# A selective scan's input: scaled by GpSimd and transposed by TensorE, in place of matmuls with a diagonal matrix

## The reference, cut to what matters

```python
x_conv = silu(causal_conv(x_in))                      # [16, 256, 256]
Bm, Cm = jnp.split(x_conv @ W_xp + b_xp, 2, axis=-1)  # 16 states each
delta = softplus(x_conv @ W_dt + b_dt)
dA  = jnp.exp(delta[..., None] * A)                   # decay
dBx = (delta * xc)[..., None] * Bm[:, :, None, :]     # drive: u times B
h = dA_t * h + dBx_t                                  # for each token t
y_t = jnp.einsum('bds,bs->bd', h, C_t)
y = y + D_skip * xc;  y = y * silu(z)
out = y @ W_out + b_out                               # then the layer norms
x = x + layernorm(x_quantized @ w_quantized.T + bias) # after a maximum over all of x
```

## Time and profile before

| | |
|---|---|
| three runs | 677.97, 679.1 and 680.75 us, median 679.1 |
| the profiled execution | 680.76 us, its span 679.0 us |
| mean granted clock of TensorE | 0.909 |
| the slots | 44.1 us to about 607 us; all but the first about 72.6 us each |
| from the end of the last scans to the end | about 72 us |
| VectorE in the slots | nine tenths busy |

### The profile page before, as it was taken

The page is one execution under the profiler, slowest core; times in us unless marked ns, Lnnn a source line. Parts: engine busy times, 40 slices in busy tenths (PEclk is TensorE's granted clock), DMA queues, the critical chain, the costliest instruction groups (busy, mean ns, idle before and its releaser), DMA issues.

```text
span 679.0 us, 10276 instructions
## 1 busy us (share of the span) xinstructions
PE 559.0 (82%) x2893; PEld 429.9 (63%) x2893; DVE 576.2 (85%) x1106; ACT 416.4 (61%) x814; POOL 322.5 (47%) x331
## 2 busy tenths in 40 slices
PE   4889999997999799986999699979997887773371
PEld 3467787775777577775777567767776776662120
DVE  4057898899998989899989998999989998985595
ACT  2447875785667757776478457765777654621364
POOL 3033554545555536455454654553655545431264
PEclk7979999997999899998999799989999899987555
DMA  7000000000000000000000000000000000000012
GB/s 208 9 1 1 0 1 1 1 0 1 1 1 1 0 2 0 0 0 0 0 0 0 0 1 0 0 0 0 0 0 0 1 1 0 1 1 0 0 47 77
DMA packets 9959, 6.20 MB, mean 9 GB/s; under 512 B 2624, under 2 KB 8896, under 8 KB 9920
## 3 DMA queue, kind: packets, MB, share of 16 engines
q1 hardware_dynamic: 9920, 5.78, 3.1%
HBM read 3.68 MB, written 2.10 MB: 9 GB/s over the span
## 4 chain that ended last, share of the span: by engine, by line
PE 42%; DVE 33%; issue 14%; ACT 5%; POOL 4%; DVEq 1%; DMA 0%; POOLq 0%; ACTq 0%
PE drive L951 16%; DVE state L1162 12%; PE hT L967 8%; PE fbank L894 7%; DVE acc_d L1185 4%; PE fbank L910 2%; PE bbank L985 2%; DVE delta L1145 2%; DVE acc_d L1182 2%; DVE yv L1191 1%; PE drive L894 1%; DVE yg L1196 1%; DVE bst L1205 1%; POOL state L592 1%; ACT h L622 1%
## 5 line engine op out<-in xcount | busy, mean ns | idle before, releaser
L1162 DVE TENSOR_TENSOR_SCAN state<-decay,drive 128x512 f32<-128x512 f32 x256 | 297.1, 1201 | 19.4 <-PE drive L951 18.2
L951 PE MATMUL drive<-diag,uT 128*128 128x256 f32 x1024 | 253.4, 392 | 1.6 <-DVE state L1162 1.0
L951 PEld LDWEIGHTS drive<-diag,uT 128*128 128x128 f32 x1024 | 193.2, 199 | 29.1 <-issue 3.3
L711 ACT ACTIVATE decay<-delta,a_neg 128x510 f32<-128x510 f32 x256 | 169.5, 723 | 20.3 <-DVE state L1162 19.2
L967 PE MATMUL hT<-ident,state 128*128 128x128 f32 x1024 | 147.4, 284 | 36.6 <-DVE acc_d L1185 35.3
L967 PEld LDWEIGHTS hT<-ident,state 128*128 128x128 f32 x1024 | 122.6, 147 | 67.5 <-issue 51.6
L729 ACT ACTIVATE term<-hT,Ct 128x256 f32<-128x256 f32 x256 | 102.6, 478 | 55.3 <-PE hT L967 55.3
L497 POOL TENSOR_SCALAR_AFFINE_SELECT diag<-Bt 128x512 f32<-128x512 f32 x128 | 98.1, 776 | 61.4 <-PE drive L951 40.8
L1185 DVE SCALAR_TENSOR_TENSOR acc_d<-hT,Ct,acc_d 128x256 f32<-128x256 f32 x224 | 92.2, 467 | 0.9 <-PE hT L967 0.9
L512 POOL TENSOR_TENSOR acc<-acc,term 128x512 f32<-128x512 f32 x48 | 61.1, 1272 | 46.6 <-ACT term L729 46.6
L527 POOL TENSOR_TENSOR bstd<-bvar,minus_half 128x4 f32<-128x4 f32 x16 | 16.3, 1017 | 107.2 <-DVE bvar L1253 62.6
(11 more groups left out here) (165 smaller groups left out, 613.3 us busy)
## 6 DMA issues: line engine op xcount, KB each, us to landing
out_dram<-state SPq DMA_DIRECT2D x8, 256.0 KB, 2.2
x_all<-in_L_attn_x_dram SPq DMA_DIRECT2D x2, 256.0 KB, 4.5
state<-in_L_attn_conv_w_dram SPq DMA_DIRECT2D x1, 512.0 KB, 5.8
w_in<-in_L_attn_W_in_dram SPq DMA_DIRECT2D x1, 256.0 KB, 3.1
w_dt<-in_L_attn_W_dt_dram SPq DMA_DIRECT2D x1, 256.0 KB, 5.0
w_out<-in_L_attn_W_out_dram SPq DMA_DIRECT2D x1, 128.0 KB, 3.5
w_ffn<-in_L_ffn_weight_dram SPq DMA_DIRECT2D x1, 64.0 KB, 2.6
bout_r<-in_L_attn_b_out_dram SPq DMA_DIRECT2D x1, 64.0 KB, 3.3
```

The lines of the kernel that those rows point to most:

```text
L711: last = nc.scalar.activation(decay[:, g % DECAYS, h, :, s, 1:], delta[:, par, h, :, 1:], ACT.Exp, scale=a_neg[:, h, SG * g + s:SG * g + s ...
L951: last = nc.tensor.matmul(dst[:, :, P * c:P * c + P], uT[:, par, TC * b + c, P * h:P * h + P], diag[:, n % DIAGS, c, :, :], start=True, st ...
L1162: nc.vector.tensor_tensor_scan(state[:, n % STATES, h, :, :].rearrange("p s t -> p (s t)"), decay[:, g % DECAYS, h, b, :, :].rearrange("p ...
```

## The change

The diag(B) blocks go. GpSimd now multiplies `uT` itself by B: for each unit four tensor_scalar instructions of 128 x 256 (two halves of time, two states), with one value of B for each partition. The result, `scaled`, has time on the partitions, four buffers as before. TensorE transposes it with the identity, 8 transposes of 128 x 128 for a unit, straight into the drive buffers. GpSimd therefore waits for `uT` before a pair's first unit, and ScalarE must not overwrite `uT` before the last unit of its old pair has been scaled. `scaled` is twice as large as `diag`; `term` goes from four buffers to two. All four step tables are set anew.

```diff
-DECAYS, DIAGS, STATES, TERMS = 2, 4, 4, 4
+DECAYS, SCALED, STATES, TERMS = 2, 4, 4, 2
...
-POOL_STEPS = dict(front_root=(0,), front_residual=(19,), sum_states=(8,), back_root=(15, 21, 26))
+POOL_STEPS = dict(front_root=(3,), front_residual=(23,), sum_states=(6,), back_root=(13, 21, 26))
...
-                 front_uT=(42, 46), back_norms=(33, 41, 47))
+                 front_uT=(45, 45), back_norms=(33, 41, 47))
...
                 if n == 0:
                     pool.wait_ge(bc_ready, nth(pr, 3, 2))
-
-                old = trailing(pr, par, n, DIAGS)
+                    pool.wait_ge(uT_ready, nth(pr, 2, 2))
+
+                old = trailing(pr, par, n, SCALED)
...
-                b_cols = Bt[:, par, g, b, :, :].rearrange("p c s -> p (c s)").unsqueeze(2).to_broadcast([P, TC * SG, P])
-                nc.gpsimd.affine_select(out=diag[:, n % DIAGS, :, :, :].rearrange("p c s t -> p (c s) t"), in_=b_cols,
-                                        compare_op=ALU.is_equal, fill=0.0, base=0, pattern=[[0, TC * SG], [-1, P]],
-                                        channel_multiplier=1).then_inc(diag_ready, 1)
+                for c in range(TC):
+                    for s in range(SG):
+                        last = nc.gpsimd.tensor_scalar(scaled[:, n % SCALED, c, s, :], uT[:, par, TC * b + c, :],
+                                                       Bt[:, par, g, b, c, s:s + 1], None, ALU.mult)
+                last.then_inc(scaled_ready, 1)
...
             def front_uT(pr, par, k):
                 act.wait_ge(front_full, nth(pr, 9, 8 + k))
+                if pr.after(2):
+                    act.wait_ge(scaled_ready, nth(pr.plus(-1), UNITS, 0))
...
-                    dst = drive[:, n % 2, h, :].rearrange("p (s t) -> p s t", s=SG)
                     for c in range(TC):
-                        last = nc.tensor.matmul(dst[:, :, P * c:P * c + P], uT[:, par, TC * b + c, P * h:P * h + P],
-                                                diag[:, n % DIAGS, c, :, :], start=True, stop=True)
+                        for s in range(SG):
+                            last = nc.tensor.transpose(drive[:, n % 2, h, L * s + P * c:L * s + P * c + P],
+                                                       scaled[:, n % SCALED, c, s, P * h:P * h + P], ident[:, :])
```

More of the change, by code:

```diff
@@ L75 @@
 ROUND_AT = 1.5 * 2.0 ** 20
-POOL_STEPS = dict(front_root=(0,), front_residual=(19,), sum_states=(8,), back_root=(15, 21, 26))
-ACT_STEPS = dict(front_xin=(5, 10), silu_table=(21,), front_silu=(21, 22, 23), exp_table=(23,),
-                 front_norm=(16,), front_xnT=(23,), front_dt=(29, 30), front_exp=(35,), front_log=(35,),
-                 front_uT=(42, 46), back_norms=(33, 41, 47))
[L86 to L90, removed]
+POOL_STEPS = dict(front_root=(3,), front_residual=(23,), sum_states=(6,), back_root=(13, 21, 26))
+ACT_STEPS = dict(front_xin=(7, 11), silu_table=(21,), front_silu=(21, 22, 23), exp_table=(23,),
+                 front_norm=(14,), front_xnT=(23,), front_dt=(27, 31), front_exp=(35,), front_log=(35,),
+                 front_uT=(45, 45), back_norms=(33, 41, 47))
+PE_STEPS = dict(front_in=(1, 6, 17, 21), front_transpose=(23,), front_dt=(24, 28), front_bc=(36,),
+                front_ut=(41, 41), back_y=(12, 15), back_out=(20,), back_transpose=(46,))
+DVE_STEPS = dict(front_stats=(0,), front_shift=(3,), front_low=(21,), front_bc=(24,), front_delta=(24,),
+                 front_u=(25,), back_y=(8, 10), back_gate=(11,), back_norms=(11, 13, 15, 21, 24, 27, 29),
+                 back_amax=(30,), back_h2T=(30,))
 def due(steps, name, at):
@@ L212, in build_sandwich @@
         decay = sb("decay", [P, DECAYS, HALVES, PAIR, SG, L])
[L213 removed]
+        scaled = sb("scaled", [P, SCALED, TC, SG, DI])
         state = sb("state", [P, STATES, HALVES, SG, L])
@@ L312, in build_sandwich @@
         decay_ready = sem("decay_ready")
-        diag_ready = sem("diag_ready")
+        scaled_ready = sem("scaled_ready")
         drive_ready = sem("drive_ready")
@@ L485, in front_residual, with scale_b @@
                     .then_inc(xnb_ready, 1)
-            def diag_b(pr, par, n):
+            def scale_b(pr, par, n):
                 g, b = n // PAIR, n % PAIR
@@ L546, in slot @@
                     if units == UNITS and n + LEAD < units:
-                        diag_b(pr, par, n + LEAD)
+                        scale_b(pr, par, n + LEAD)
                     elif front:
-                        diag_b(pr.plus(1), 1 - par, n + LEAD - units)
+                        scale_b(pr.plus(1), 1 - par, n + LEAD - units)
                     steps_at(pr, par, 2 * n, front, back)
@@ L574, in _ @@
             front_root(Pair(1))
+            front_residual(Pair(0), 0)
             for n in range(LEAD):
-                diag_b(Pair(0), 0, n)
-            front_residual(Pair(0), 0)
+                scale_b(Pair(0), 0, n)
             slot(Pair(0), 0, True, False)
```

5 lines of the change are left out of this document (1 added, 4 removed).

## The result

The changed kernel took 824.5 us (median of 4 runs, 824.17 to 825.49) against 678.54 us for the kernel before on the same chip (4 runs, 677.85 to 680.75): a ratio of 1.2147, 95% interval 1.2116 to 1.2178. The forecast was 672 us in a range of 660 to 696. Both its sign and its size were wrong. The cause is the one of rival 1, GpSimd as the bound; but its price was put at 700 us, and even its upper end, 735, was too low.

A forecast was written before the change was run, and what follows sets the result against it. TensorE was taken to bound the first slot and VectorE the seven others. From 680.76 us, -4.1 - 3.9 + 0.7 - 0.7 = -8.0 gave 672.8, or 671.1 by the median; predicted 672 us, range 660 to 696.

The forecast's parts named there:

- rival 1: GpSimd becomes the bound at line 499 in every slot, slower than before; price 700 us, upper end about 735; chance 0.22.
- the price of line 499: GpSimd's new tensor_scalar of 256 elements: 450 ns, from the one-input affine_select's row, between 401 and 745 ns.
- the break-even of 0.58 us: Time T of one scaling at which GpSimd's slot, 64 T + 31, equals the about 68 us VectorE's slot leaves.
- 64 T + 31 us: GpSimd's time in a slot: 64 scalings of T each, plus its other work and hold-ups by VectorE; about 59 of 72.
- The sum of the rivals: The rivals' way to a whole time: 680 us plus 7.75 slots times a slot's excess over 72.6 us.
- Drive waits of the later slots: VectorE's waits for TensorE's drive in the seven later slots vanish: -4.1 us together.
- first slot: Drive waits in the slot without back steps: 5.5 of 9.4 us stay, -3.9 us; bounds 0 and -9.4.
- The start: Before VectorE's first scan: GpSimd's four scalings add 1.8 us, TensorE's part shortens by about 1.1; +0.7 us.
- The moved steps: bshift's wait saves 1.1 us a slot; amax_p and the copy behind it wait 0.7 and 0.3 more; -0.7 in all.
- The two-microsecond wait for the output projection stays: VectorE's wait of 7 times 2.1 us unchanged, since gate and residual stand at place 11 in both tables.
- The locks: VectorE's two-input instructions and GpSimd holding each other up: counted as nothing, between -0.7 and +2 us a slot.
- Rival 3: TensorE pauses more often and its clock falls; if it stayed low, a slot takes 84 us, the whole 768; chance 0.02.

The follow-up runs named there:

- run 1: GpSimd alone, no other engine at work, five of each instruction form; the one-operation tensor_scalar of 256 elements took 922 ns, 847 with a constant.
- run 6: The changed kernel with a second operation, plus 0, in each tensor_scalar, nothing else; 692.38 us, 1.0197 of the kernel before.
- run 12: Kernel before, old places, drive by 8 transposes of uT; GpSimd makes diag(B) unread, without waiting for uT; 673.13 us, ratio 0.9895.
- run 10: run 6 with two of VectorE's norm steps moved one place: residual sum later, third bshift earlier; 667.81 us, 0.984 of the kernel before.

## Why the prediction was wrong, step by step

**The step that failed is the price of line 499**, "I take 450 ns, by the row of the same kind with one input", with 401 to 745 ns as its bounds. It measured 953 in the kernel and 922 alone. The row of two elements (222 ns) gave the fixed part well: it is a lone multiply with a constant, and run 1's line through 847 ns for 256 elements ends at 207 + 2 x 2.5 = 212. But a row of two elements knows nothing of the rate, and I took the rate from another instruction. The upper bound, from the two-input add, failed as well: one input can be dearer than two, and here it is, 2.50 ns an element against the 2.06 of the add. With one of two ends of the bounds beyond the break-even of 0.58 us, and no row of that instruction at any size but 2, rival 1 with 0.22 had too small a chance. (Its own terms at 745 ns add up to about 741 us, not 735.)

The Trainium skill, "GPSIMD Engine Reference", section 3.1, led to an estimate of 603 ns, which the prediction set aside for the affine_select's row. It was on the right side of the break-even and still a third below the 922 ns of run 1; section 4.1's roughly line-rate for one input does not hold for this form, whose 256 elements took longer than those of the two-input product (922 against 722 ns).

**The step that carried it over was right.** The prediction had a slot bound by GpSimd as 64 T + 31 us. With the measured T that is 61.0 + 31 = 92.0 us; the slot above has 91.69. The parts agree less closely than the sum: GpSimd's other work there is 27.1 us and its idle time 3.6, where the 31 stood for work and for being held up by VectorE. The sum of the rivals, 680 + 7.75 x (92.0 - 72.6), gives 830 us, and 824.5 were measured; rival 1's further 2 us a slot for the roots would have made it some 844, too much. The break-even is borne out from one side (498 ns in run 6: GpSimd 481.0 us busy, and no longer the bound); the point itself was not tried.

**A second part failed beside it: the sum at the right price.** In run 6 line 499 takes 498 ns, under the break-even, and the time is 692.4 us, not 672. In VectorE's waits of 119 to 610 us the forecast had 4.8 us less (-4.1 and -0.7); they are 12.8 us more: 9.3 at `res`, 4.6 and 2.9 at `amax_p` and the copy behind it, and 7.6 for TensorE's transposes of the states, before `acc_d` (4.1) and before the scans (3.5), which the forecast did not have, against -7.9 at `bshift` and -3.7 at the drive. So a right price of the instruction alone would not have made the 672 right either; the clock at the projection and the states' transposes stood in the sum at nothing.

**Drive waits of the later slots, -4.1 us; first slot, -3.9 us.** Run 12 isolates them. In the later slots the wait is gone, as forecast. In the first slot 2.3 us are left of the 9.4, a gain of 7.1 and not 3.9. That run has the old places; with the new ones 2.3 us are left in run 6 too, and 5.2 in run 10, near the 5.5 of the forecast. From 42 to 60 us the granted clock was 1.00 in run 6 and 0.83 in run 10. The projection's wait took 2 us back, and the end came 6.6 us earlier by the spans. TensorE's saving is in the rows: eight transposes in 1.04 us for 1.89, 147.4 us of drive instead of 253.4 in run 12.

**The start, +0.7 us.** Measured +1.5 (45.58 against 44.08). `uT` was there 1.4 us earlier (40.43 against 41.82), which I had missed; GpSimd's four scalings took 3.7 us where I had put 1.8. In run 6 the first scan starts at 42.95, 1.1 us before the old one, in run 10 at 44.00.

**The moved steps, -0.7 us.** `bshift`'s 7.9 us do go in run 6. The waits at `amax_p` and the copy behind it come, 4.6 + 2.9 us, as forecast (0.7 and 0.3 a slot). What I did not see is the output projection: "The two-microsecond wait for the output projection stays" was wrong by 9 us in run 6, and what made it wrong is the clock in those matmuls, not their place.

**The locks, 0.** Right. From before to after the mean of `delta` fell from 1904 to 1337 ns; `u` rose from 1209 to 1393, the gate from 1224 to 1300, the two on `nrm` from 680 and 692 to 768 and 779. VectorE was busy for 573.6 us, before 576.2.

**Rival 3, the clock.** The mean fell to 0.792 after, but TensorE was waiting for GpSimd. In run 12, with as many transposes and no such wait, it was 0.87 and the time shorter than before: transposes in place of products do not keep the clock low, as the earlier trace rows said. But in stretches the lower level came and cost time, as the rival had it and the sum did not: 9.2 us at the projection in run 6, 2.0 in run 12, 4.8 after.

## What to carry to other kernels

Before work is given to an engine that does not have it yet, measure that very instruction there, in its form and size: at 922 ns, far over the break-even, this forecast would have been a loss. Price what can't be measured by the rate of a row with the same operations, not by the number of its inputs, and when one of several such prices lies beyond the break-even, give the engine's becoming the bound its full chance. When a slot is full on one engine, look for its lateness at all the dates that it keeps, and retune the places after the instruction is right, not before.

## What the runs showed of the hardware

- GpSimd, float32, 128 x 256: tensor_scalar with one operation 922 ns with a scalar for each partition, 847 with a constant; multiply then add or multiply then multiply 478 and 479 with the former, 404 with constants; maximum then add 1066; tensor_tensor 722, copy 399. With a neutral second operation (add 0.0 or multiply by 1.0) the multiply with a scalar for each partition takes 0.52 of its time.
- One tensor_tensor of 1024 elements with both inputs repeated by zero steps takes 1892 ns alone (line 76), four lone scalings of the same work 4 x 922 = 3688, four two-operation ones 4 x 478 = 1912.
- The same 16 matmuls of the projection took 2.05 us or 3.58 us (clock 1.00 and 0.57) in kernels that differ in two of VectorE's steps, each by one place, and in one and the same kernel from slot to slot (three of seven slow in the changed kernel); the cause stays open.
